# A layer pair on one core: the first key group in plain form, the second weights loaded earlier, and a flag computed by TensorE and VectorE

## What is computed

```python
x = x + tanh(g_xattn[0]) * xattn0(layernorm(x), ctx, mask, bias, ...)   # 32 heads of 128
x = x + tanh(g_ffn[0])   * ffn0(layernorm(x), qweight, lut4, lut8, b)
x = x + tanh(g_xattn[1]) * xattn1(layernorm(x), ctx, ...)               # 32 query, 8 key heads
x = x + tanh(g_ffn[1])   * ffn1(layernorm(x), weight, bias)

# xattn0: keys and values from the context, queries from the RMS-normed input
h_k = ctx @ w_k.T ; h_v = ctx @ w_v.T          # 1024 tokens x 512 -> 4096 each
score = softmax(h_q @ h_k.T + position_bias, masked) ; out = (score @ h_v) @ w_out.T

# ffn0: weights from 4-bit codes, or 8-bit codes for tokens with a large norm
y = where(norm(x) > 64.0, x @ w_8bit.T, x @ w_4bit.T) + bias
```

## Time and profile before

| | |
|---|---|
| median of 3 runs | 1759.9 us (1759.55 to 1760.72) |
| the profiled execution | 1761.1 us, its span 1759.3 us |
| TensorE busy | 1700.4 us (97%) |
| VectorE, ScalarE, GpSimd busy | 1154.6, 852.3, 564.2 us |

### The profile page before, as it was taken

One profiled execution on the slowest core, in us unless ns is written; L12 is line 12 of the kernel. 1 busy time (PEld: TensorE's weight loads), 2 busy tenths in 40 slices (PEclk: granted clock), 3 DMA queues, 4 the chain that ended last, 5 costly groups with the idle time before them and its releaser, 6 DMA issues.

```text
span 1759.3 us, 31142 instructions
## 1 busy us (share of the span) xinstructions
PE 1700.4 (97%) x11024; PEld 1539.1 (87%) x11024; DVE 1154.6 (66%) x2063; ACT 852.3 (48%) x2254; POOL 564.2 (32%) x537
## 2 busy tenths in 40 slices
PE   5999999989999999999879999999999999999998
PEld 4999999978999999999658898989898989898997
DVE  7433343789777777779966666575756667575576
ACT  4333443544445444454415555555555555555553
POOL 6233222253222222222332232333333323233243
PEclk8999999999999999999989999999999999999999
DMA  4444443532333233332201001000100000010001
GB/s 178 179 157 158 152 158 143 185 124 91 113 104 107 93 110 107 104 108 72 96 1 37 25 25 37 12 24 24 36 24 24 36 12 28 20 36 15 1 1 48
DMA packets 62346, 132.29 MB, mean 75 GB/s; under 512 B 5200, under 2 KB 40400, under 8 KB 59216
## 3 DMA queue, kind: packets, MB, share of 16 engines
q1 hardware_dynamic: 62288, 131.52, 21.8%
HBM read 95.85 MB, written 35.65 MB: 75 GB/s over the span
## 4 chain that ended last, share of the span: by engine, by line
PE 89%; DVE 5%; issue 2%; POOL 1%; ACT 1%; DMA 1%; SPq 0%; DVEq 0%; POOLq 0%
PE bank L1597 20%; PE bank L1599 19%; PE bank L1598 19%; PE bank L1645 17%; PE bank L1769 3%; PE bank L1916 3%; PE bank L1726 3%; PE bank L1935 2%; PE bank L1714 1%; PE bank L1817 1%; PE bank L1940 1%; DVE stats L999 0%; DVE idx L1184 0%; PE bank L1614 0%; DVE residual L1213 0%
## 5 line engine op out<-in xcount | busy, mean ns | idle before, releaser
L628 POOL TENSOR_TENSOR p<-p,rn 128x512 f32<-128x512 f32 x128 | 131.1, 1045 | 244.7 <-DVE rn L1473 244.7
L568 POOL TENSOR_TENSOR pr<-pr,rn 128x512 f32<-128x512 f32 x64 | 66.6, 1041 | 369.0 <-DVE rn L1223 369.0
L1597 PE MATMUL bank<-w_hi,xt_hi 128*128 (+2 forms) x512 | 177.6, 347 | 0.0
L1599 PE MATMUL bank<-w_hi,xt_lo 128*128 (+2 forms) x512 | 172.5, 337 | 0.0
L1598 PE MATMUL bank<-w_lo,xt_hi 128*128 (+2 forms) x512 | 171.4, 335 | 0.0
L1597 PE MATMUL bank<-xt_hi,w0q_hi 128*128 128x256 f32 x512 | 149.4, 292 | 0.0
L914 ACT ACTIVATE p<-bank,nb,q_r 128x256 f32<-128x256 f32 x256 | 141.0, 561 | 11.5 <-DVE nb L1469 4.8
L1598 PE MATMUL bank<-xt_lo,w0q_hi 128*128 128x256 f32 x512 | 143.9, 281 | 0.0
L1599 PE MATMUL bank<-xt_hi,w0q_lo 128*128 128x256 f32 x512 | 143.9, 281 | 0.0
L821 ACT ACTIVATE ptr<-bank 128x512 f32<-128x512 f32 x63 | 37.6, 597 | 215.8 <-PE bank L1714 215.8
L490 POOL TENSOR_TENSOR q_r<-q_ms,half 128x4 f32<-128x4 f32 x64 | 64.4, 1007 | 210.1 <-DVE q_ms L1449 210.1
(11 more groups left out here) (215 smaller groups left out, 5572.2 us busy)
## 6 DMA issues: line engine op xcount, KB each, us to landing
stage<-w SPq DMA_DIRECT2D x35, 512.0 KB, 3.3
keys_of_layer<-kout SPq DMA_DIRECT2D x16, 1024.0 KB, 4.4
values_of_layer<-vout SPq DMA_DIRECT2D x16, 1024.0 KB, 4.8
kt<-keys_of_layer SPq DMA_DIRECT2D x64, 256.0 KB, 3.1
vs<-values_of_layer SPq DMA_DIRECT2D x64, 256.0 KB, 2.8
kraw<-wk SPq DMA_DIRECT2D x16, 512.0 KB, 5.1
vraw<-wv SPq DMA_DIRECT2D x8, 1024.0 KB, 7.0
stage0q<-w SPq DMA_DIRECT2D x16, 512.0 KB, 3.7
```

The lines of the kernel that those rows point to most:

```text
L568: pool.tensor_tensor(by4(pr), by4(pr), rn[:, :].unsqueeze(2).to_broadcast([P, 4, P]), ALU.mult).then_inc(norm_done, 1)
L628: pool.tensor_tensor(p1[:, half_p:half_p + 2, :], p1[:, half_p:half_p + 2, :], rn1[:, half_p:half_p + 2].unsqueeze(2).to_broadcast([P, 2, ...
L1597: nc.tensor.matmul(out_ap, l_hi, r_hi, start=(c == 0), stop=False)
L1599: op = nc.tensor.matmul(out_ap, l_lo, r_hi, start=False, stop=(c == n - 1))
```

## The change

It has five parts.

1. The first key job (group 0) is computed as four plain quarters, each from two block products of 6 matmuls: 48 matmuls in place of 42, by the new `first_products`. They need the four raw quarters of the weight and of the context, and neither sums nor differences. A21 is rounded into S2's place (`FIRST_A21`). ScalarE copies each finished quarter (`first_keys`); there is no `part1`, `part2`, `part4` nor addition by VectorE for this job.
2. T1 to T4 are all made by VectorE and counted by one semaphore `diff_done`; GpSimd makes no sums for group 0. The start orders of ScalarE and VectorE are new: all four context quarters come first, T4 comes last, after the late value part.
3. SP loads the second group's weights ahead of the waits for the last stores and ahead of `qw` and `lut`.
4. In the attention slots of layer 0, the weight's rounding moves behind `output_hi` on ScalarE, and its low part behind `output_lo` on VectorE, in all slots that have them.
5. The maximum over partitions: VectorE spreads `any_hi` over 128 columns of `pr`, TensorE transposes these (after `low_ffn(2)`), and VectorE reduces the result and casts it. GpSimd's `partition_all_reduce` is gone.

```diff
+        FIRST_A21 = S2
+        FIRST_BANK = ((0, 1), (2, 6))
...
# SP
             load_values(0, 1)
+            for w in range(2):
+                sp.wait_ge(w_lo_done[w], 1)
+                load_weight(w, 1)
             sp.wait_ge(kd_out, 16 * NG)
             sp.wait_ge(vd_out, 16 * NG)
...
-            for w in range(2):
-                sp.wait_ge(w_lo_done[w], 1)
-                load_weight(w, 1)
...
# GpSimd
-            weight_sums(kraw, kraw_in, ksum_done, 0)
-            pool.wait_ge(ctx_in[1], 16)
-            pool.wait_ge(ctx_in[2], 16)
-            pool.wait_ge(ctx_in[3], 16)
-            pool.tensor_tensor(traw[:, T3, :, :], craw[:, 3, :, :], craw[:, 1, :, :], ALU.subtract).then_inc(diff34_done, 1)
-            pool.wait_ge(diff12_done, 2)
-            pool.tensor_tensor(traw[:, T4, :, :], craw[:, 2, :, :], traw[:, T2, :, :], ALU.subtract).then_inc(diff34_done, 1)
-            weight_sums(vraw, vraw_in, vsum_done, 0)
+            weight_sums(vraw, vraw_in, vsum_done, 0, 0)
...
-            pool.wait_ge(any_done, 1)
-            pool.partition_all_reduce(any_hi[:, 1:2], any_hi[:, 0:1], P, bass.bass_isa.ReduceOp.max).then_inc(all_done, 1)
             first_low(2)
...
# ScalarE, start
+            def first_keys(n, m):
+                act.wait_ge(product_done, 2 * n + m + 1)
+                nc.scalar.activation(kout[:, m, n, :], bank[FIRST_BANK[n][m]][:, :],
+                                     ACT.Copy).then_inc(((c11_done, c21_done), (c12_done, c22_done))[n][m], 1)
+            act.wait_ge(kraw_in, 16)
+            nc.scalar.activation(kw_hi[:, A22:A12 + 1, :, :], kraw[:, A22:A12 + 1, :, :], ACT.Copy).then_inc(kw_hi_done, 1)
+            nc.scalar.activation(kw_hi[:, FIRST_A21, :, :], kraw[:, A21, :, :], ACT.Copy).then_inc(kw_hi_done, 1)
             context_hi(0, 0)
             context_hi(1, 0)
+            context_hi(0, 1)
             context_hi(1, 1)
             values_early(0)
+            difference_hi(T2)
+            first_keys(0, 0)
+            first_keys(0, 1)
+            difference_hi(T3)
+            difference_hi(T1)
+            values_late(0)
+            difference_hi(T4)
+            first_keys(1, 0)
+            first_keys(1, 1)
...
# ScalarE, slot
+                exponentials(i + 1)
+                if not (last and j == BODY - 1):
+                    queries_out(i + 2)
+                if not (first and j == 0):
+                    output_hi(i, j - 1)
                 if p in (0, 2) and not (last and j >= 4):
                     w = p // 2
                     act.wait_ge(w_in[w], 16 * (n + 2))
                     wait(act, (q_ps, y_ps)[w], 4 * n)
                     nc.scalar.activation(w0_hi[w][1 - parity][:, :], stage0[w][:, :], ACT.Copy).then_inc(w_hi_done[w], 1)
-                exponentials(i + 1)
-                if not (last and j == BODY - 1):
-                    queries_out(i + 2)
-                if not (first and j == 0):
-                    output_hi(i, j - 1)
...
# VectorE, start (low parts and differences)
+            context_lo(0, 1, 3)
             dve.wait_ge(ctx_in[0], 16)
             dve.wait_ge(ctx_in[1], 16)
+            difference(T1, craw[:, 1, :, :], craw[:, 0, :, :])
+            context_lo(1, 1, 4)
             dve.wait_ge(ctx_in[3], 16)
+            dve.wait_ge(diff_done, 1)
+            difference(T2, craw[:, 3, :, :], traw[:, T1, :, :])
+            difference(T3, craw[:, 3, :, :], craw[:, 1, :, :])
             values_early_lo(0)
+            difference_lo(T2, 5)
+            difference_lo(T3, 6)
+            difference_lo(T1, 7)
+            values_late_lo(0)
+            dve.wait_ge(ctx_in[2], 16)
+            dve.wait_ge(diff_done, 2)
+            difference(T4, craw[:, 2, :, :], traw[:, T2, :, :])
+            difference_lo(T4, 8)
...
# VectorE, slot: the low part moves from behind accumulate() to here
                 if lag1:
                     output_lo(i, (j - 1) % 2)
+                if p in (0, 2) and not (last and j >= 4):
+                    w = p // 2
+                    dve.wait_ge(w_hi_done[w], n + 2)
+                    nc.vector.tensor_tensor(w0_lo[w][1 - parity][:, :], stage0[w][:, :],
+                                            w0_hi[w][1 - parity][:, :].bitcast(fp32), ALU.subtract).then_inc(w_lo_done[w], 1)
...
# VectorE, flag
                     dve.wait_ge(any_done, 1)
+                    nc.vector.tensor_copy(pr[:, 0:P], any_hi[:, 0:1].to_broadcast([P, P])).then_inc(all_done, 1)
...
-            dve.wait_ge(all_done, 1)
+            dve.wait_ge(any_ps, 1)
+            nc.vector.tensor_reduce(any_hi[:, 1:2], TB[:, 0:P], axis=AX.X, op=ALU.max).then_inc(any_done, 1)
+            dve.wait_ge(any_done, 2)
             nc.vector.tensor_copy(flag[:, :], any_hi[:, 1:2]).then_inc(flag_done, 1)
...
# TensorE
+            def first_products(n):
+                for k in range(2):
+                    x_hi, x_lo = quarter(ct_hi, k, n), quarter(ct_lo, k, n)
+                    blocks = ((0, (A11, A12)[k]), (1, (FIRST_A21, A22)[k]))
+                    pe.wait_ge(t_hi_done, 2 * n + k + 1)
+                    if n == 0 and k == 0:
+                        pe.wait_ge(kw_hi_done, 2)
+                    for m, a in blocks:
+                        for c in range(2):
+                            nc.tensor.matmul(bank[FIRST_BANK[n][m]][:, :], kw_hi[:, a, c, :], x_hi[:, c, :],
+                                             start=(k == 0 and c == 0), stop=False)
...
-                for k in range(4):
+                for k in range(1 if first else 0, 4):
                     products_early(s, k)
...
             low_ffn(2)
+            pe.wait_ge(all_done, 1)
+            pe.wait_ge(pt_done, U)
+            nc.tensor.transpose(TB[:, 0:P], pr[:, 0:P], ident[:, :]).then_inc(any_ps, 1)
             transpose_rows(1, 6)
```

More of the change, by code:

```diff
@@ L307, in nth @@
             if isinstance(job, int) and job <= 0:
-                return (1, 2, 8, 9, 5, 3, 4)[product - 1] if job == 0 else 0
+                return 4 if job == 0 else 0
+            if isinstance(job, int) and job == 1 and product < 3:
+                return 4 + product
             if isinstance(job, int) and job == 4 * SG - 1 and product in (3, 4):
-                return 7 * job + 3 + product
-            return 7 * job + (-1, 0, 8, 9, 5, 3, 4)[product - 1]
+                return 7 * job + product
+            return 7 * job + (-4, -3, 5, 6, 2, 0, 1)[product - 1]
         job_out = lambda k, m, n: kout[:, m, n, :] if k % 2 == 0 else vout[:, n, :, m, :]
@@ L504, in _, with weight_sums @@
             pool.wait_ge(half_done, 1)
-            def weight_sums(raw, raw_in, done, m):
+            def weight_sums(raw, raw_in, done, m, earlier):
                 pool.wait_ge(raw_in, 16 * (m + 1))
@@ L752, in projections @@
                 part1(s, 1)
-                quarter12(s, 0)
+                if not first:
+                    quarter12(s, 0)
                 keys_early(2 * s + 1)
@@ L1086, in projections @@
                 last = isinstance(s, int) and s == SG - 1
-                quarter11(s, 0)
                 if not first:
+                    quarter11(s, 0)
                     quarter21(s - 1, 3)
-                else:
-                    values_late_lo(0)
-                    context_lo(0, 1, 8)
-                quarter22(s, 0)
-                if not first:
+                    quarter22(s, 0)
                     values_late_lo(s)
@@ L1103, in projections @@
                 quarter11(s, 1)
-                quarter21(s, 0)
+                if not first:
+                    quarter21(s, 0)
                 keys_early_lo(2 * s + 1)
@@ L1249, in slot @@
                     accumulate(i - 2, 2 * ((j - 3) % 4))
-                if p in (0, 2) and not (last and j >= 4):
-                    w = p // 2
-                    dve.wait_ge(w_hi_done[w], n + 2)
-                    nc.vector.tensor_tensor(w0_lo[w][1 - parity][:, :], stage0[w][:, :],
-                                            w0_hi[w][1 - parity][:, :].bitcast(fp32), ALU.subtract).then_inc(w_lo_done[w], 1)
                 if first and j == 0:
@@ L1681, in products_last @@
                 job = 4 * s + k
-                first = isinstance(s, int) and s == 0 and k == 0
-                if first:
-                    pe.wait_ge(t_lo_done, 7)
-                pe.wait_ge(part4_done, job + 1)
+                if isinstance(s, int) and s == 0 and k == 1:
+                    pe.wait_ge(t_lo_done, 8)
+                pe.wait_ge(part4_done, job)
                 product(3, k, 0, False).then_inc(product_done, 1)
@@ L1692, in projections @@
                 last = isinstance(s, int) and s == SG - 1
[L1693 removed]
+                for k in range(1 if first else 0, 4):
                     products_early(s, k)
[L1695 removed]
+                    if k == 0:
+                        products_last(s - 1, 3)
+                    elif not (first and k == 1):
                         products_last(s, k - 1)
[L1697 to L1698 removed]
```

95 lines of the change are left out of this document (43 added, 52 removed).

## The result

The changed kernel takes 1750.3 us (median of 4 runs, 1750.07 to 1750.49) against 1760.2 for the kernel before beside it: a ratio of 0.9944, 95% interval 0.9927 to 0.9961. That is 9.9 us faster where the forecast said 14.6; it lies within the range, near its upper end, and by the number alone rival 2's 1750.9 is nearer than the forecast's 1745.3. The profiled execution has a span of 1748.7 (before 1759.3), so its rows have to account for 10.6.

A forecast was written before the change was run, and what follows sets the result against it. TensorE, busy 97% of the span with some 59 us idle, was taken as the bound; only work it waits for counts. 4.1 + 1.3 + 9.2 = 14.6 us off the median of 1759.9 gives 1745.3, range 1738.5 to 1752.5.

The forecast's parts named there:

- rival 2: Whole kernel: start gains only 2, turn 0, flag 7 with TensorE slow in row 3; 1750.9 us; chance 0.18.
- Part A: Kernel start: TensorE restarts at 33.8, second key group starts at 40.2; gain 4.1 us, bounds 2 and 10.
- Part B: Turn to layer 0 attention and slot order: 2.8 us won, 1.5 lost; net gain 1.3, bounds -0.5 and 3.
- In slots 4 and 6 the exponentials are done before VectorE gets there, so the order is neutral: Layer 0 attention, slots 4 and 6: the new order of the weight's low part costs VectorE nothing.
- the slot 2 of the prediction: Layer 0 attention, VectorE: low part waits for `w0o_hi`, ends at 376.6 instead of 375.1; costs 1.5 us.
- Rival 4: Slots with a weight: residual sum over 1.15 us later delays TensorE's output projection, 17 us lost, 1762 or 1779; chance 0.04.
- Part C: First feed-forward: without the all-reduce GpSimd's 13.6 us stand goes; layer 1 starts 9.2 us earlier, bounds 7 and 12.1.
- products of rows 3 to 5 as before: First feed-forward, TensorE: after 888.2 these products take 10.07 us as in the kernel before, to 898.3.
- z_mid ... at 898.2: First feed-forward: normalised rows meet the last weight part (to 897.7), are there at 898.2, TensorE's transpose at 898.4.
- the lower bound of 7: First feed-forward: gain only 7 us if the new 3 us pause before 888.2 makes row 3 slow.
- The upper bound of 12.1 for free gates: First feed-forward: gain 12.1 us if the gate operations aren't held up by GpSimd.
- its own signs: Whole kernel: wrong if slots grow, TensorE restarts before 30 or after 36, or another GpSimd pause appears.

The follow-up runs named there:

- Experiment 9: Changed kernel with ScalarE's rounding of T4 moved behind the copy of the first value part: 1746.2 us, ratio 0.9920 to the kernel before.
- experiment 4: Kernel before with only the new start (plain first key group, differences on VectorE): 1756.2 us, ratio 0.9973 to the kernel before.
- experiment 2: Changed kernel with the second group's two weight loads put back behind the waits for the last stores, new slot order kept: 1751.5 us.
- experiment 7: Changed kernel with ScalarE's old order in all slots but the first, VectorE keeping the new one: 1749.2 us, ratio 0.9942 to the kernel before.
- experiment 6: Changed kernel with the new slot order in the first slot only, the old order in all later slots: 1745.4 us, ratio 0.9914 to the kernel before.
- 5: Kernel before with only the earlier weight loads and the new slot order of ScalarE and VectorE: 1761.8 us, ratio 1.0006 to the kernel before.
- the second kernel of 8: Changed kernel with GpSimd held until the gates are computed and its third and fifth weight parts moved later: 1742.9 us, ratio 0.9902 to the kernel before.
- experiment 1: Changed kernel with the old order of ScalarE and VectorE inside the slots, early loads kept: 1746.8 us, ratio 0.9917 to the kernel before.
- experiment 3: Kernel before with only the flag made by TensorE and VectorE in place of the all-reduce: 1753.5 us, ratio 0.9958 to the kernel before.
- experiment 8: Changed kernel with GpSimd waiting until the gates are computed, in two kernels: the wait alone 1748.1 us, with weight parts also moved 1742.9 us.

## Why the prediction was right and where it was wrong

**Part A, right.** VectorE's operations beside the value sums took 2.31 (2.30 taken), the three low parts 5.65 in all (5.3), the late value part 3.34 (2.81), T4 1.74 (1.21); T4 was done at 30.78, TensorE restarted at 33.57, and the lead is 4.27 (4.1). Two pieces were off against each other: three operations met value sums, not four, and the last two each took 0.53 more. Experiment 9 shows that the end of VectorE's queue, through ScalarE's, was the right bound; experiment 4 that the part stands alone (a lead of 3.5 there).

**Part B, the turn right, the slots wrong.** The exponentials came free by the order alone (experiment 2) and TensorE gained 2.83 (2.8). The step that failed is "In slots 4 and 6 the exponentials are done before VectorE gets there, so the order is neutral", and with it the net gain of 1.3, which measured -1.1. The reading behind it was wrong at the start: the prediction has TensorE never waiting in the 64 slots, but in the kernel before it waited 2.2 us in all for VectorE's residual sum, 0.72 and 0.70 of them in the first eight slots. Each row below is the time between two of VectorE's score operations; it is the same to 0.02 in the changed kernel and in experiment 7, and the same to 0.02 before and in experiment 6:

| from sc | to sc | old place of the low part | new place | difference |
|---|---|---|---|---|
| 3 | 4 | 7.40 | 9.14 | +1.74 |
| 4 | 5 | 7.58 | 7.58 | 0 |
| 5 | 6 | 9.78 | 10.76 | +0.98 |
| 6 | 7 | 7.58 | 8.44 | +0.86 |
| 7 | 8 | 8.71 | 9.68 | +0.97 |
| 8 | 9 | 8.41 | 8.42 | +0.01 |

The first is the slot 2 of the prediction (1.5 forecast; the idle times 0.65, 0.52 and 0.25 are there, and the low part takes 1.87 beside GpSimd's addition of mask and bias). That 1.5 came near is in part luck: the prediction's reason, a low part that waits for `w0o_hi`, is gone in experiment 7, and the slot still takes 9.14, as the low part then stands longer beside GpSimd.

The others were not seen. In slot 4 the low part takes 1.68 where it took 1.22, and the shift behind it 3.26 where it took 2.75; both now fall beside GpSimd's addition, where in the old order only the shift did (together 0.97). Slot 6 has the low part at 1.68 and the mask operation at 2.18 (1.22 and 1.68 in experiment 6). The 0.86 in between comes through TensorE's clock: behind its wait of 2.49 for the late residual sum it was granted 0.57 (393 to 397), so its next scores were late and VectorE waited 0.90 for them. This 0.86 stands where the clock fell: in experiments 2 and 5 and the second kernel of 8 it is between 4 and 5, behind the first long wait (granted clock 0.66 in 374 to 377 in the second kernel of 8), and 6 to 7 takes 7.58 or 7.57. In experiment 6, with waits of 0.7, the clock stayed at 1.00 in both places. In sum 4.6 instead of 1.5. That the low part, the shift and the mask operation grow by the meeting with GpSimd is read from the timelines; no run moved GpSimd's addition alone.

Rival 4 named this very place, VectorE's residual sum against TensorE's output projection, but looked for it in the ordinary slots, where VectorE has slack. There TensorE was busy for 160.00 of 160 us, and behind the ninth scores the lead went from 3.40 to 3.10 only (the old order lost nothing: 6.45 to 6.42 in experiment 1). It decided in the first eight slots, where VectorE has none.

**Part C, right in kind, too large in size.** The gate operations waited for GpSimd as said, row 6's transposes moved to 888.0 (experiment 3; 888.2 forecast), no pause came back. The term mis-sized is what follows: "products of rows 3 to 5 as before" took 0.9 us more, because TensorE's clock had dropped in its wait (granted 0.84 over these rows, 1.00 before: the mechanism that the lower bound of 7 carried), and "z_mid ... at 898.2" was met by a weight part for longer, a wait of 1.30 where 0.1 was taken. With 0.2 for the earlier 888.04, 9.2 - 0.9 - 1.2 + 0.2 is 7.3; the rows say 7.4. The upper bound of 12.1 for free gates was too low: experiment 8 reaches 13.7, as row 3 then also runs at full clock and the z rows are free.

**Sum.** Forecast 4.1 + 1.3 + 9.2 = 14.6. The rows: 4.2 - 1.1 + 7.4 = 10.5, of a span that fell by 10.6. The medians moved 9.9. Rival 2, whose 1750.9 is nearest, had the flag right (7, and TensorE slow in row 3) but took 2 for the start and 0 for the turn where 4.2 and -1.1 were measured; its two misses cancel. By its own signs the prediction was wrong in one place, as slots did grow, the first eight; and the `z_mid` wait that it put under 1 us was 1.30.

The page of the Trainium skill on SBUF ("SBUF — State Buffer", section "SBUF: two separate sides") says that a VectorE operation with two SBUF inputs (against a GpSimd operation that reads SBUF) or in a 2-port mode, and a GpSimd operation, exclude each other for the whole instruction. The runs agree and show how small an operation it hits: with two inputs of 128x4 elements 1.23 us beside a GpSimd addition of 1.27, and 0.16 without it. `gate_hi`, 2.29 us beside a weight part of 2.36 and 0.17 without it, reads one tensor; whether it ran in such a mode no run shows.

The 6 us that the Trainium skill ("GPSIMD Engine Reference", section "Instruction dispatch") gives for the first call of a freshly loaded kernel do not cover what the all-reduce cost: taking it away alone won 7.36 us although it added a block of 2.3 us in the gates. The pause of 5.88 ahead of it is near that figure; the 7.39 behind it is a second one.

## What to carry to other kernels

Where an engine has no slack, moving one of its operations within its queue is not neutral even if every input is ready: it takes away the filler of a wait and changes what runs beside GpSimd, and a TensorE that then waits longer can lose clock on top. Compare the period of the full engine over several slots with both orders. Count the small VectorE operations on a critical chain too, and keep GpSimd idle while they run: one wait of GpSimd won 3.4 us in the feed-forward here. When a copy that releases TensorE stands in a queue behind something that needs the end of another queue, move it ahead (3.3 us by one line).

## What was not expected of the hardware

- The same instructions in the same order gave second key groups from 39.2 to 40.8 in the profiled runs of kernels with the changed start (39.22, 39.59, 39.62, 39.84, 40.08, 40.35, 40.46, 40.84). Three of them ran on one chip (39.22, 40.46, 40.84). That it is the loads, for which the start waits, was not tested. A single profile's lead carries about a microsecond of this, while VectorE's 54.0 us over six slots repeat to 0.03.
- A wait of 2.5 us at the turn was followed in some runs by about 3.4 us of granted clock 0.50 (after: mean 0.83 in 350 to 360, which is 3.4 of 10 us at half) and in others by none (1.00 in experiments 7 and 9). In the same way the clock fell behind the first of the two long waits of the first slots in some runs and behind the second in others. What decides it was not tested.
